# A graph layer on one core: seven combinations side by side in float32, one cast and one subtraction a pair, and weights, biases and adj loaded and used in another order

## The reference

```python
h = jnp.maximum(_layernorm(x, axis=-1), 0.0)
mask = (adj > 0).astype(x.dtype)
deg = jnp.sum(mask, axis=1, keepdims=True)
agg = mask @ h / jnp.maximum(deg, 1.0)
combined = jnp.concatenate([h @ W_self + b_self, agg @ W_nb + b_nb], axis=-1)
out = x + relu(combined @ W_comb + b_comb)
```

## Time and profile before

| | us |
|---|---|
| median of 3 runs | 914.53 (914.16 to 917.45) |
| profiled execution | 915.82 |
| its span | 914.0 |
| TensorE busy | 896.9 (98%) |
| VectorE busy | 799.1 (87%) |
| ScalarE busy | 377.5 (41%) |
| GpSimd busy | 91.0 (10%) |

### The profile page before, as it was taken

How to read it: one execution, slowest core, us unless ns; L and a number is a source line. 1 busy time by engine, 2 the same in 40 slices (tenths; PEclk the granted TensorE clock), 3 DMA queues, 4 the chain that set the end, 5 groups by cost and what they waited for, 6 DMA issues and landing times. The chain is left out here.

```text
span 914.0 us, 19105 instructions
## 1 busy us (share of the span) xinstructions
PE 896.9 (98%) x7720; PEld 760.1 (83%) x7720; DVE 799.1 (87%) x1512; ACT 377.5 (41%) x358; POOL 91.0 (10%) x132
## 2 busy tenths in 40 slices
PE   7999899899999999999999999999999999999997
PEld 5555478788888888888888888888888888888886
DVE  5999898898998988898889888888899998888884
ACT  3999854233333333332333333333333333333320
POOL 2888820000000000000000000000000000000000
PEclk9999999999999999999999999999999999999999
DMA  6467769999999999999999999999999999999950
GB/s 213 162 220 274 265 233 391 400 370 388 376 384 377 378 380 377 373 370 368 367 380 377 389 392 370 381 365 364 358 374 372 380 386 379 369 376 376 398 211 22
DMA packets 61367, 312.80 MB, mean 342 GB/s; under 512 B 6880, under 2 KB 8032, under 8 KB 28512
## 3 DMA queue, kind: packets, MB, share of 16 engines
q1 hardware_dynamic: 60736, 311.06, 87.7%
q10 hardware_dynamic: 544, 0.52, 0.2%
HBM read 294.78 MB, written 16.78 MB: 341 GB/s over the span
## 5 line engine op out<-in xcount | busy, mean ns | idle before, releaser
L625 PE MATMUL banks<-t,operands 128*128 128x257 f16 x7168 | 786.5, 272 | 2.6 <-DVE work L757 2.6
L625 PEld LDWEIGHTS banks<-t,operands 128*128 128x128 fp8e4 x7168 | 698.3, 97 | 90.7 <-issue 2.8
L468 ACT ACTIVATE mask<-stage,few 128x2048 fp8e4<-128x2048 int32 x128 | 252.7, 1999 | 415.5 <-DVE turned L720 318.9
L705 DVE TENSOR_SCALAR mask<-stage 128x2048 uint8<-128x2048 int32 x128 | 154.5, 1226 | 5.8 <-DMA stage<-in_adj_dram 5.8
L565 PE MATMUL banks<-t,xh 128*128 128x512 f16 x384 | 89.3, 383 | 4.2 <-DVE t L698 3.1
L757 DVE TENSOR_TENSOR work<-banks,work 128x512 f32<-128x512 f32 x32 | 22.1, 692 | 74.8 <-ACT work L518 74.8
L734 DVE TENSOR_TENSOR operands<-turned,operands 128x1024 uint32<-128x1024 uint32 x64 | 78.4, 1225 | 8.8 <-DVE turned L720 0.5
L714 DVE STREAM_TRANSPOSE operands<-mask 128x512 uint32<-128x512 uint32 x128 | 83.1, 687 | 0.2 <-DVE t L693 0.2
L720 DVE STREAM_TRANSPOSE turned<-mask 128x512 uint32<-128x512 uint32 x128 | 80.8, 669 | 0.0
L736 DVE TENSOR_TENSOR operands<-turned,operands 128x1024 uint32<-128x1024 uint32 x64 | 78.2, 1222 | 0.0
L565 PEld LDWEIGHTS banks<-t,xh 128*128 128x128 f16 x384 | 37.7, 98 | 44.0 <-issue 4.6
(11 more groups left out here) (62 smaller groups left out, 391.4 us busy)
## 6 DMA issues: line engine op xcount, KB each, us to landing
stage<-in_adj_dram SPq DMA_DIRECT2D x256, 1024.0 KB, 8.5
out_dram<-operands SPq DMA_DIRECT2D x32, 256.0 KB, 2.8
xh<-in_x_dram SPq DMA_DIRECT2D x32, 256.0 KB, 9.5
own<-out_dram SPq DMA_DIRECT2D x32, 256.0 KB, 10.5
out_dram<-xh SPq DMA_DIRECT2D x32, 256.0 KB, 6.0
t<-in_x_dram SPq DMA_DIRECT2D x30, 256.0 KB, 4.4
turned<-in_x_dram SPq DMA_DIRECT2D x2, 256.0 KB, 5.4
t<-in_L_gnn_W_nb_dram ACTq DMA_DIRECT2D x1, 256.0 KB, 4.0
```

Of the source, the lines that this page charges most:

```text
L468: act.activation(mask[:, b, :].bitcast(FP8), stage[:, b, :], ACT.Sigmoid, bias=steep, scale=STEEP, saturate=False).then_inc(formed_s, 1)
L625: mm = pe.matmul(banks[:, n, 0:width], bytes_of[:, c, :, s], t16[:, KQ * h + SUB * c + s, SLOT[n], 0:width], start=(h == 0 and c == 0 and ...
L705: dve.tensor_scalar(mask[:, b, :], stage[:, b, :], 0.0, float(MINUS_ONE_BYTE), ALU.is_gt, ALU.mult).then_inc(formed_v, 1)
```

## The change

- One buffer `kept[j % 3]` of 1408 float32 now holds `own` (512) and the seven combinations z side by side (7 x 128); two of them lie in `operands`, the third in `work`. `evict` writes in that order, `combine` writes its three into places 4 to 6, ScalarE casts all seven in one instruction, VectorE subtracts all seven in one. Columns of w12 are reordered, so the moving operand of the second tile's matmuls is two blocks of 256 columns.
- `evict(j)` waits for the whole of `low_of_t(j - 3)`; `combine` no longer waits for `low_of_t`.
- WARM is 22. SP loads the biases right after x pairs 0 and 1. The copies b_wide are done by GpSimd, in front of root_of(0). The negation is done in two pieces. VectorE does low_of_h(0), w_low(0) and low_of_h(1) ahead of the statistics of pairs 2 and 3. ScalarE does high_of_h(1) in the setup.
- TensorE: after the W products the constant, then project(0), project(1), turns 2 and 3, project(2), turn 4, project(3), turn 5, project(4), turns 6 and 7, project(5), turn 8, and so on.
- The steps of adj loads, forms and turns are changed as in the tables; make_third(2) is done ahead of merge_a(0).

```diff
-WARM = 16
+WARM = 22
-FORM_STEPS_S = {20: A12, 22: A21}
-FORM_STEPS_V = {23: A22, 25: A11}
-TURN_STEPS_V = {24: A22, 26: A11}
+FORM_STEPS_S = {20: A12, 23: A21}
+FORM_STEPS_V = {19: A22, 21: A11}
+TURN_STEPS_V = {20: A22, 22: A11}
-NEXT_STEPS_V = {27: A22, 28: A11}
+NEXT_STEPS_V = {25: A22, 28: A11}
-LOAD_STEPS = {12: A12, 14: A21, 16: A22, 18: A11}
-NEXT_LOADS = {21: (1, A12), 23: (1, A21), 24: (1, A22), 26: (1, A11), 28: (2, A22), 29: (2, A11)}
+LOAD_STEPS = {10: A22, 11: A11, 13: A12, 15: A21}
+NEXT_LOADS = {20: (1, A22), 22: (1, A11), 23: (1, A12), 25: (1, A21), 27: (2, A22), 29: (2, A11)}
+TURNS_AFTER = {1: (2, 3), 2: (4,), 3: (5,), 4: (6, 7)}
...
             load_x(0)
             load_x(1)
+            sp.dma_start(b_cols, b_cols_in[:, :]).then_inc(b_loaded, DONE)
+            sp.dma_start(bc_row, b_comb.rearrange("(a n) -> a n", a=1).partition_broadcast(P)).then_inc(b_loaded, DONE)
             sp.dma_start(ws_t, w_self_t.rearrange("(h p) n -> p h n", p=P)).then_inc(w_loaded[0], DONE)
...
-                if j >= RING:
-                    pool.wait_ge(t_low, 2 * (j - RING + 1))
-                pool.tensor_tensor(c[:, 0, :], z[:, 6, :], z[:, 1, :], ALU.subtract).then_inc(apart_ready, 1)
+                pool.tensor_tensor(z[:, 4, :], z[:, 2, :], z[:, 1, :], ALU.subtract).then_inc(apart_ready, 1)
...
+            pool.wait_ge(b_loaded, 2 * DONE)
+            for m in range(2 * HALVES):
+                pool.tensor_copy(b_wide[:, m, :], b_cols[:, m:m + 1].to_broadcast([P, P])).then_inc(wide_ready, 1)
             root_of(0)
+            pool.wait_ge(sum_high, 1)
+            pool.tensor_scalar(w12[:, 0, :, W_MINUS:W_WIDE], w12[:, 0, :, W_SUM:W_F1], -1.0, None, ALU.mult
+                               ).then_inc(sum_negated, 1)
             pool.wait_ge(sum_ready, 1)
-            pool.tensor_scalar(w12[:, :, :, W_MINUS:W_WIDE], w12[:, :, :, W_SUM:W_F1], -1.0, None, ALU.mult
+            pool.tensor_scalar(w12[:, 1, :, W_MINUS:W_WIDE], w12[:, 1, :, W_SUM:W_F1], -1.0, None, ALU.mult
                                ).then_inc(sum_negated, 1)
...
             def high_of_t(j):
-                act.wait_ge(evicted, j + 1)
-                act.activation(direct_in_t(j, 0), direct(j), ACT.Copy).then_inc(t_high, 1)
                 act.wait_ge(combined, j + 1)
-                act.activation(t16[:, j, DIRECT:7, 0:P], combos[:, j % RING, 0:3, :], ACT.Copy).then_inc(t_high, 1)
+                act.activation(t16[:, j, :, 0:P], kept_z(j), ACT.Copy).then_inc(t_high, 1)
...
+                                       w12[:, w, half, :].rearrange("p (a n) -> p a n", a=3)[:, 0:2 + t:1 + t, :],
...
             def low_of_t(j):
-                dve.wait_ge(t_high, 2 * j + 1)
-                dve.tensor_tensor(direct_in_t(j, P), direct(j), direct_in_t(j, 0), ALU.subtract).then_inc(t_low, 1)
-                dve.wait_ge(t_high, 2 * j + 2)
-                dve.tensor_tensor(t16[:, j, DIRECT:7, P:D], combos[:, j % RING, 0:3, :], t16[:, j, DIRECT:7, 0:P],
-                                  ALU.subtract).then_inc(t_low, 1)
+                dve.wait_ge(t_high, j + 1)
+                dve.tensor_tensor(t16[:, j, :, P:D], kept_z(j), t16[:, j, :, 0:P], ALU.subtract).then_inc(t_low, 1)
...
             low_of_h(0)
+            w_low(0)
+            low_of_h(1)
             for p in range(2, 4):
                 stats_of(p)
-            w_low(0)
+            dve.wait_ge(c_product, 1)
+            dve.tensor_tensor(c_row[:, :], pair_ps[2][:, 0, 0:D], bc_row, ALU.add).then_inc(c_ready, 1)
             shifts(1)
...
             make_first(2)
             make_second(2)
+            make_third(2)
```

More of the change, by code:

```diff
@@ L149, in x_pair, with kept_z @@
             return flat_t[:, p * PLACE:p * PLACE + 4 * D].bitcast(F32)
[L152 to L164, removed]
+        KEPT = 2 * D + 7 * P
+        slot_1 = operands[:, 1, :, :].rearrange("p o w -> p (o w)").bitcast(F32)
+        kept = [slot_1[:, 0:KEPT], slot_1[:, KEPT:2 * KEPT], work[:, :, :, :].rearrange("p n c m -> p (n c m)")[:, 0:KEPT]]
+        def kept_z(j):
+            return kept[j % RING][:, 2 * D:KEPT].rearrange("p (c m) -> p c m", c=7)
         w_sum = own[:, 0, 0, :].rearrange("p (h m) -> p h m", h=HALVES)
         w_second = own[:, 0, 1, :].rearrange("p (h m) -> p h m", h=HALVES)
-        combos = work
         flat_work = work[:, :, :, :].rearrange("p n c m -> p (n c m)")
@@ L319, in store_own @@
                 sp.wait_ge(evicted, j + 1)
-                sp.dma_start(out[j, :, :].rearrange("p (t d) -> p t d", t=2), kept_blocks(j)[:, 2:6, :].rearrange("p (t f) m -> p t (f m)", t=2)
-                             ).then_inc(own_stored[j % RING], DONE)
+                sp.dma_start(out[j, :, :], kept[j % RING][:, 0:2 * D]).then_inc(own_stored[j % RING], DONE)
             def load_again(r):
@@ L422, in _ @@
                         norm(j + 3, t)
+                if j == 0:
+                    root_of(2)
                 if j >= 1:
@@ L493, in _ @@
             w_high_half(0)
+            high_of_h(1)
             for t in norms_s(2):
@@ L580, in _ @@
                 turn(j)
-            project(0)
             pe.wait_ge(wide_ready, 2 * HALVES)
@@ L586, in _ @@
             mm.then_inc(c_product, 1)
-            turn(2)
-            for j in range(1, PAIRS):
-                if j + 2 < PAIRS:
-                    turn(j + 2)
+            for j in range(PAIRS):
                 project(j)
+                for n in TURNS_AFTER.get(j, (j + 3,) if j >= 5 else ()):
+                    if n < PAIRS:
+                        turn(n)
             def product(r, h, n):
@@ L852, in _ @@
                 norm(2, t)
-            dve.wait_ge(b_loaded, 2 * DONE)
-            for m in range(2 * HALVES):
-                dve.tensor_copy(b_wide[:, m, :], b_cols[:, m:m + 1].to_broadcast([P, P])).then_inc(wide_ready, 1)
             for p in range(4, 6):
@@ L899, in _ @@
                 outer_sums(r)
-                if r == 0:
-                    make_third(2)
                 if i < STEPS:
```

41 lines of the change are left out of this document (17 added, 24 removed).

## The result

The changed kernel took 918.57 us (median of 14 runs, 916.85 to 921.25), the kernel before 914.21, run beside it (14 runs, 912.58 to 917.45): a ratio of 1.005 with the interval 1.0038 to 1.0062, so slower by 0.5%. I had forecast 911.6; the time lies 1.6 us above 917.0, the upper end of the range that was to hold in 8 cases of 10.

The account below looks back on a forecast made before the run. TensorE was taken to bound the kernel in the pair and adj stages, leaving setup, end of the pair stage and one pause to win. 0.5 + 2.4 + 0 = 2.9, so 914.5 - 2.9 = 911.6 us, range 906.8 to 917.0.

Parts of the forecast that it names:

- the opening: Setup to project(5): W1's low half moved ahead wins 1.6 us at project(2), some 0.5 us left at project(5).
- the seven combinations in one buffer: Pair stage: one cast and one subtraction each save about 0.08 us a pair, worth nothing while TensorE sets the pace.
- the forms: End of the pair stage: adj moved up wins 1.1 us on VectorE's wait and 1.3 on ScalarE's forms, +2.4 us.
- the pause: Adj stage, 2.6 us wait: moving make_third(2) wins zero, as DMA throughput sets the landing; bounds -0.6 and 2.6 us.
- All four signs of being wrong: project(5) before 33.5 or after 36; middle pairs over 3.05 us; low clock at 10-15 us; adj pause outside 2-3 us.
- The biases: Opening: root_of(0) waits for the bias row, landing at 7.4 to 7.6 us, and four GpSimd copies of 1.1 us.
- D: Opening: how much later root_of(0) starts than before, taken as 1.7 us, bounds 0 and 3.0.
- rival B: Opening: bias row is the new wait, D 3.0, TensorE at 1.2 GHz, project(5) 3.3 us later; 915.4 us, chance 0.17.
- VectorE's chain: Opening: VectorE becomes the bound, low_of_h(2) at 23.3 us behind six pairs' statistics, project(2) at 24.1 us.
- Rival C: Pair stage: GpSimd becomes the bound, three operations stretched 0.17 us each, 3.6 us over 30 pairs; 918 us, chance 0.08.
- WARM 22: Setup: six more transposes cost 0.1 us, may bring W products to full rate; worth nothing, as turn(0) waits for norms.
- The matmul in two blocks: Pair stage: two blocks of 256 columns in place of 512 taken at 0, bounds 0 and 0.003 us a matmul.

Follow-up runs that it names:

- experiment 1: Changed kernel with GpSimd's root_of(0) moved ahead of its wait for the biases and their copies; 915.83 us, ratio 1.0019 to the kernel before.
- 3: Changed kernel with root_of(0) ahead of the bias copies and VectorE's subtraction in two pieces; 912.75 us, ratio 0.9993 to the kernel before.
- 5: Changed kernel with root_of(0) first, two subtractions and ScalarE's cast in two pieces as well; 912.72 us, ratio 0.9975.
- 6: Changed kernel with root_of(0) first, two subtractions and the old tables of adj loads, forms and turns; 915.77 us, ratio 1.0011.
- 10: Changed kernel with root_of(0) first, two subtractions, old tables, and SyncE issuing two adj blocks before waiting for the last stores; 911.64 us, ratio 0.9977.
- 11: The kernel of 10 with WARM 16 in place of 22; 912.1 us, ratio 0.9976.
- 7: Changed kernel with root_of(0) first, two subtractions, and low_of_h(2) ahead of the statistics of pairs 6 and 7 on VectorE; 915.83 us, ratio 1.0009.
- experiment 2: Changed kernel with VectorE's one subtraction done in two pieces of 512 and 384 columns, the one cast kept; 915.46 us, ratio 1.0026.
- 12: Kernel before with only the new tables of adj loads, forms and turns; 913.09 us, ratio 0.999.
- 9: Kernel before with SyncE issuing adj blocks (2, A12) and (2, A21) ahead of its wait for the last stores and load_again(0); 912.37 us, ratio 0.9982.
- 4: Kernel before with only make_third(2) moved ahead of merge_a(0); 915.82 us, ratio 1.0013.

## Why the prediction was wrong, step by step

In the prediction's own terms it had +0.5 for the opening, 0 for the seven combinations in one buffer, +2.4 for the forms and 0 for the pause, +2.9 in all. The profiles have -2.40, -3.57, +0.41 and +2.73, which is -2.83. The step that failed most is the second, the single subtraction put at nothing. All four signs of being wrong came: project(5) at 37.34, pairs of 3.28 us in the middle (45.94 / 14), a granted clock of 0.58 over 11.86 to 15.00, and no pause of 2 to 3 us.

**The biases: the mechanism was right, the landing too early.** root_of(0) did run behind copies that wait for b_comb. The four copies took 1.00 (1.1 forecast). The row landed at 8.49 and not at 7.4 to 7.6, so D was 2.43 where I took 1.7. In the two profiles of this order it is 2.43 and 1.88 (root_of(0) at 9.46 and 8.91), beside the point of about 2.5 that I gave rival B, and B's signs are in the trace: over 3 us of idle TensorE, then products at 1.2 GHz (3.14). B priced project(5) at 3.3 us later than before; it was 2.40. (By the prediction's own steps B should have said 2.8: a loss of 0.8 for D = 3.0, and 2.0 for the slow products.)

**VectorE's chain and what is left at project(5).** With D = 1.7 and the full clock I had low_of_h(1) starting at 14.6 and low_of_h(2) at 23.3. They came at 16.53 and 25.54, because the slow products hold low_of_h(1) and six pairs' statistics stand behind it. I had 1.6 us won at project(2) and 0.5 at project(5); the trace has 0.55 lost and 2.40 lost, the low clock of project(2) included. This "+0.5" was -2.4, and experiment 1 gets it back. Even with root_of(0) early the reordering gives little: project(5) starts at 33.90 on average over the six profiles with root first (1, 3, 5, 6, 10, 11; 7 has another edit there), and at 34.57 over the five that keep the opening of before. That is 0.67 us, where I had put 1.6 for D = 0. The giving back at turn(7) was understated, as experiment 7 shows.

**"It is worth nothing there": the step that failed most.** I saved 0.08 us a pair on VectorE and counted the middle as TensorE's, with 0 for the one piece. It cost 3.57 us over 14 pairs in the profile, and experiment 2 puts it at 3.35. In the medians the step from experiment 1 to 3, the same edit, is 3.1 us. Rival C had the cause, VectorE's instruction holding GpSimd's, and the place, and I gave it 0.08, because the port is held less in total. Its size is luck: C spread 3.6 us over 30 pairs, with all three operations of a pair stretched until GpSimd is the bound. The trace has 3.57 in 14 pairs, and TensorE stands there only behind the norm that follows the root, four times, for 1.31, 0.49, 0.49 and 0.51 us. The total was the wrong measure: VectorE's busy time in the middle did fall, from 41.76 to 38.69, and TensorE still lost. What counts is how long VectorE holds a GpSimd instruction that is next to be waited for. The Trainium skill, "GPSIMD Engine Reference", section "Key points", has VectorE instructions with two SBUF inputs contend with GpSimd; this trace agrees, with 1.47 us for a norm of 0.56 beside the 1.08 us subtraction.

The profiles fall into three groups by the norm behind the root, which turn(n) needs next. With the single piece (after, 1) it takes 1.47 and the middle 45.94 and 45.14. With two pieces and the same lead of 0.12 (6, 7, 11) it takes 1.07, no wait of TensorE shows in the middle, and that takes 43.05 to 43.32 (43.05 in 7, whose tables are those of after and 1), although the mean of all norms is no smaller (1.03 to 1.06 against 0.98). With two pieces and a lead of 0.21 (2, 3, 10) it takes 0.56 and the middle 42.56 to 42.59. (In 5 both leads occur, with 42.81.) So most of the loss is the length of the piece, and up to 0.8 us is the lead. What sets the lead, 0.12 or 0.21, stays open, and so does whether a single piece with a lead of 0.21 would cost anything; I made no experiment that moves the root alone.

**The forms "+2.4": it did not come, and that the pause gave nearly as much is luck.** VectorE's wait before step 28 went, but the pair stage did not become shorter by the tables. From project(20) to S the seven profiles with the new tables (after, 1, 2, 3, 5, 7, 12) take 38.94 to 40.39, 39.5 on average, and the seven with the old 38.05 to 39.68, 38.6 on average: longer if anything, though within the scatter of 1.6. In the changed kernel itself a single wait of 2.31 us stands at 101.82. The gain there is 0 at best, and not 2.4.

**The pause "zero": wrong, and so was its reason.** From a DMA share of 0.98 I had concluded that throughput sets the landing. The share is real, but it is that of a window from S + 17 on. The delay arose ahead of it, where the DMA engines stood idle while SyncE waited for the last stores, and load_again(0) then moved beside (2, A12); all later blocks of ScalarE came behind that. Getting load_again(0) out of the way takes most of the pause: the new tables, with which the last stores land sooner after S (12: 0.46), or the order of two lines (9: 0.81). With make_third(2) moved as well, 0 to 0.57 is left (0 in after, 2, 7, 10 and 11, 0.57 in 1), so that move may bring the last half microsecond; alone it stays unproven (4). So 2.7 us were won in the adj stage, and this hid half of what the opening and the middle lost: 2.40 + 3.57 - 0.41 - 2.73 = 2.83 in the profiles, 4.36 in the medians.

The 1.5 us between these two sums are the executions': the profiled one of before took 915.82, 1.6 above its median, that of after 918.65, which is its median but for 0.1.

**WARM 22 and the one cast at nothing:** right within 0.5 us (11, 5). A slip in the working: from 1.60, 3.68 and six transposes at 0.21 end at 6.5 and not 6.3; they ended at 6.11. **The matmul in two blocks at nothing:** right, 42.56 to 42.59 for 14 pairs in experiments 2, 3 and 10, against 42.37: 0.2 us.

## What to carry to other kernels

Do not judge a merged instruction by the busy time it saves on its own engine: look at which short instruction of another engine runs beside it, which of the two starts first, and who waits for the short one. A copy put in front of the instruction that releases everything is paid from the landing of its data, and the idle stretch that it opens can then cost a second time through the clock. A pause under a DMA share near 1 is still worth a look at the issuing queue: what is issued just ahead of the transfer that lands last, did the engines stand idle before that, and must it go first?

## What the hardware showed that I had not expected

- One VectorE subtraction of 128x896 (1.08 us) holds a GpSimd norm that started 0.12 us ahead of it for its whole length: 0.56 us becomes 1.47 (45.73 with 45.85, and 58.52 with 58.65). A norm that started 0.18 us ahead is not held, and the subtraction takes 1.32 (51.02 with 51.20). Cut into 512 and 384 columns the subtraction stretches combines from 0.45 to 0.89 (experiment 2).
- Two pieces in a row can hold a norm as long as one: with leads of 0.00 to 0.088 us it took 1.45 to 1.51, with 0.12 it ended between them after 1.07 (experiments 5, 6, 7, 11).
- GpSimd's root, an operation on 8 columns, took 1.65 and 2.44 us in the middle, three to four times a norm of 256 columns.
- GpSimd copies 128x128 float32 from a broadcast column in 0.296 us (L405, four alike).
- The granted clock after an idle stretch is not a matter of its length alone. After 2.64 us before project(2) of the changed kernel it was 0.50, after 2.79 us in experiment 1 the twelve matmuls ran in 2.76, at full rate. In the changed kernel TensorE had run at 1.2 GHz and stood 3.10 us shortly before; in experiment 1 it had stood 0.77.
- The same kernel's stage starts shift by up to 1.6 us from one execution to the next (S 120.02 and 118.44), nearly all of it after project(20) and in the opening, none in the 14 pairs between (42.37 and 42.38).
